# Gated cross-attention with a quantised feed-forward on one core: blocks of tokens as the outer order, groups of heads as the inner one, and split weights kept in DRAM

## The reference, cut to what matters

```python
# x, ctx: 32 sequences x 64 tokens x 512;  32 heads of 128 in 8 groups of 4 heads, one K and V head a group
x = x + tanh(g_xattn) * attn(layernorm(x), ctx)          # causal, softmax over 64 keys
#   Q = xn @ Wq.T (512 -> 4096)   K, V = ctx @ Wk.T, ctx @ Wv.T (512 -> 1024)   y = attn @ Wd.T (4096 -> 512)
x = x + tanh(g_ffn) * (layernorm(x) @ dequant(qweight).T + bias)     # 6-bit weights, 512 -> 512
```

## Time and profile before

| | |
|---|---|
| Time, median of 3 runs | 1126.22 us (1125.69 to 1127.69) |
| Time of the profiled execution | 1125.69 us |
| Span of its profile | 1123.9 us |
| Instructions | 20957 |
| PE busy | 1052.4 us, 94% |
| DVE, ACT, POOL busy | 748.5, 488.8, 109.0 us |
| Mean granted TensorE clock | 0.982 |
| DMA | 53.29 MB, 47 GB/s on average |

### The profile page before, as it was taken

One profiled execution on the slowest core, in us unless ns is written; L12 is line 12 of the kernel. 1 busy time (PEld: TensorE's weight loads), 2 busy tenths in 40 slices (PEclk: granted clock), 3 DMA queues, 4 the chain that ended last, 5 costly groups with the idle time before them and its releaser, 6 DMA issues.

```text
span 1123.9 us, 20957 instructions
## 1 busy us (share of the span) xinstructions
PE 1052.4 (94%) x8060; PEld 594.7 (53%) x8060; DVE 748.5 (67%) x1391; ACT 488.8 (43%) x938; POOL 109.0 (10%) x163
## 2 busy tenths in 40 slices
PE   5799799999999999999999999999999999999985
PEld 2455455555555555555555555555555555555442
DVE  5666467766756566665746666665756576787978
ACT  4666553434433543434433543334433543435342
POOL 1423210000000000000000000000000000003565
PEclk9899899999999999999999999999999999999998
DMA  8140000300021001200021001200022002100111
GB/s 318 58 150 2 19 20 13 101 20 20 20 77 57 20 19 45 76 14 19 20 77 57 20 19 38 79 18 19 20 77 57 20 19 61 35 15 7 38 57 75
DMA packets 46106, 53.29 MB, mean 47 GB/s; under 512 B 3392, under 2 KB 36160, under 8 KB 43584
## 3 DMA queue, kind: packets, MB, share of 16 engines
q1 hardware_dynamic: 46016, 51.92, 15.1%
HBM read 30.93 MB, written 4.19 MB: 31 GB/s over the span
## 4 chain that ended last, share of the span: by engine, by line
PE 77%; DVE 7%; issue 4%; ACT 1%; POOL 0%; DVEq 0%; ACTq 0%; POOLq 0%
PE pa L1085 37%; PE py L1085 27%; PE av L1176 5%; PE ps L1147 3%; PE pp L1161 2%; DVE xacc L894 1%; PE pp L1231 1%; PE pa L1224 1%; PE av L1206 1%; DVE sc L763 1%; DVE row_max L767 1%; DVE q L726 1%; DVE row_sum L776 1%; DVE sc L769 1%; DVE xacc L802 0%
## 5 line engine op out<-in xcount | busy, mean ns | idle before, releaser
L1085 PE MATMUL pa<-xT,wq 128*128 128x512 f16 x1536 | 349.1, 382 | 8.9 <-DVE q L726 5.8
L1085 PE MATMUL py<-wd,att 128*128 128x512 f16 x1536 | 352.1, 382 | 2.2 <-DVE att L793 2.2
L1085 PEld LDWEIGHTS pa<-xT,wq 128*128 128x128 f16 x1536 | 145.4, 99 | 183.4 <-issue 25.9
L1085 PEld LDWEIGHTS py<-wd,att 128*128 128x128 f16 x1536 | 149.1, 98 | 167.2 <-issue 8.1
L525 ACT ACTIVATE q<-pa 128x512 f16<-128x512 f32 x128 | 75.6, 591 | 260.9 <-PE pa L1085 260.9
L802 DVE SCALAR_TENSOR_TENSOR xacc<-py,f_y,xacc 128x512 f32<-128x512 f32 x128 | 96.0, 750 | 134.2 <-PE py L1085 134.0
L569 ACT ACTIVATE att<-av 128x256 f16<-128x256 f32 x256 | 81.0, 385 | 154.3 <-PE av L1176 154.3
L793 DVE SCALAR_TENSOR_TENSOR att<-av,att 128x256 f16<-128x256 f32 x256 | 93.8, 418 | 69.2 <-ACT att L569 69.2
L726 DVE SCALAR_TENSOR_TENSOR q<-pa,q 128x512 f16<-128x512 f32 x128 | 87.7, 685 | 46.0 <-ACT q L525 46.0
L1085 PE MATMUL pa<-wv,cT 128*128 128x128 f16 x1536 | 97.4, 221 | 2.3 <-DVE q L726 2.3
L1085 PEld LDWEIGHTS pa<-wv,cT 128*128 128x128 f16 x1536 | 91.0, 99 | 3.4 <-issue 2.7
(11 more groups left out here) (105 smaller groups left out, 999.2 us busy)
## 6 DMA issues: line engine op xcount, KB each, us to landing
v_dup<-v_nat SPq DMA_DIRECT2D x128, 128.0 KB, 2.4
raw_d<-in_wdT SPq DMA_DIRECT2D x8, 1024.0 KB, 4.9
raw_q<-in_wqT SPq DMA_DIRECT2D x7, 1024.0 KB, 4.9
shared<-in_ctxT SPq DMA_DIRECT2D x4, 1024.0 KB, 6.8
out_x<-xacc SPq DMA_DIRECT2D x16, 256.0 KB, 2.0
xacc<-in_x SPq DMA_DIRECT2D x3, 1024.0 KB, 15.7
raw_k<-in_wkT SPq DMA_DIRECT2D x8, 256.0 KB, 5.1
raw_v<-in_wvT SPq DMA_DIRECT2D x8, 256.0 KB, 5.5
```

What stands on the lines that cost most here:

```text
L1085: last = pe.matmul(out, stationary(a, i), moving(b, i), start=(i == 0 and (a, b) == PASSES[0]), stop=(i == count - 1 and (a, b) == PASSES[ ...
```

## The change

It does five things.

1. **Order.** A pass is one block through all 8 groups; there are four passes, step `n` being group `n % 8` of block `n // 8`. The hardware loop is gone: all 32 steps are written out.
2. **Weights.** Pass 0 loads and splits the weights, now those of the group after the next in each step, and writes the split fp16 tiles to DRAM (`kept_q`, `kept_k`, `kept_v`, `kept_d`). Passes 1 to 3 read them back (`back_qkv`, `back_d`). The sums of squares, the norms and the splits of one group, spread over two steps before, are all in one step.
3. **Blocks.** `xT`, `cT` and `v_dup` hold two blocks, `xacc` three, `c_raw` one. Block `tb + 1` is loaded in step 1 of a pass (`load_block`), its context is squared in step 2, its statistics are taken at the end of step 3, its norm is made in step 4 (`norm_of`), and its context is split in steps 5 and 6.
4. **Feed-forward.** The second norm of a block is in step 0 of the next pass, its feed-forward in step 1 (`ffn_of`); block 2 has it in the last step, block 3 behind it.
5. **Start.** ACT runs an exponential of one column ahead of its first wait. The first norm has four slots of `xn` and `xh` instead of three. The weights of group 1 are prepared ahead of step 0.

```diff
-        def groups(eng, step):
-
-            for tb in range(BLOCKS):
-                step(0, tb, True, False)
-            with eng.Fori(1, GROUPS - 1) as g:
-                for tb in range(BLOCKS):
-                    step(g, tb, False, False)
-            for tb in range(BLOCKS):
...
+        def norm_of(n):
+
+            g, tb = n % GROUPS, n // GROUPS
+            if g == 4 and tb < BLOCKS - 1:
+                return NORMS.index((1, tb + 1))
+            if g == 0 and tb > 0:
+                return NORMS.index((2, tb - 1))
+            return None
...
+        def ffn_of(n):
+
+            g, tb = n % GROUPS, n // GROUPS
+            if n == STEPS - 1:
+                return BLOCKS - 2
+            if g == 1 and 0 < tb < BLOCKS - 1:
+                return tb - 1
+            return None
+
...
+            def keep_qkv(g):
+
+                sp.wait_ge(wq_hi, 4 * (g + 1))
+                sp.wait_ge(wq_lo, 4 * (g + 1))
+                sp.wait_ge(wk_hi, g + 1)
+                sp.wait_ge(wk_lo, g + 1)
+                sp.wait_ge(wv_hi, g + 1)
+                sp.wait_ge(wv_lo, g + 1)
+                sp.dma_start(kept_q[g], wq[:, :, :, :, :].rearrange("p c h k n -> p (c h k n)")).then_inc(q_kept, 16)
+                sp.dma_start(kept_k[g], wk[:, :, :, :].rearrange("p c k n -> p (c k n)")).then_inc(k_kept, 16)
+                sp.dma_start(kept_v[g], wv[:, :, :, :].rearrange("p c k n -> p (c k n)")).then_inc(v_kept, 16)
+
+            def keep_d(g):
+
+                sp.wait_ge(wd_hi, 4 * (g + 1))
+                sp.wait_ge(wd_lo, 4 * (g + 1))
+                sp.dma_start(kept_d[g], wd[:, :, :, :].rearrange("p c h n -> p (c h n)")).then_inc(d_kept, 16)
+
+            def back_qkv(m):
+
+                g = m % GROUPS
+                sp.wait_ge(q_mm, 4 * m)
+                sp.wait_ge(q_kept, 16 * GROUPS)
+                sp.dma_start(wq[:, :, :, :, :].rearrange("p c h k n -> p (c h k n)"), kept_q[g]).then_inc(q_back, 16)
+                sp.wait_ge(k_mm, m)
+                sp.wait_ge(k_kept, 16 * GROUPS)
+                sp.dma_start(wk[:, :, :, :].rearrange("p c k n -> p (c k n)"), kept_k[g]).then_inc(k_back, 16)
+                sp.wait_ge(v_mm, m)
+                sp.wait_ge(v_kept, 16 * GROUPS)
+                sp.dma_start(wv[:, :, :, :].rearrange("p c k n -> p (c k n)"), kept_v[g]).then_inc(v_back, 16)
+
+            def back_d(n):
+
+                sp.wait_ge(y_mm, 4 * n)
+                sp.wait_ge(d_kept, 16 * GROUPS)
+                sp.dma_start(wd[:, :, :, :].rearrange("p c h n -> p (c h n)"), kept_d[n % GROUPS]).then_inc(d_back, 16)
...
+            for n in range(STEPS):
+                g, tb, m = n % GROUPS, n // GROUPS, n + 1
+                if n >= GROUPS:
+                    back_d(n)
+                if tb == 0 and g + 1 < GROUPS:
+                    keep_qkv(g + 1)
+                if tb == 0 and g + 2 < GROUPS:
+                    load_qkv(g + 2)
+                if g == 1 and tb + 1 < BLOCKS:
+                    load_block(tb + 1)
+                if n == GROUPS - 1:
+                    load_ffn()
+                if tb == 0:
+                    keep_d(g)
+                    if g + 1 < GROUPS:
+                        load_d(g + 1)
+                if GROUPS <= m + 1 < STEPS:
+                    back_qkv(m + 1)
+                if m < STEPS:
+                    duplicate_v(m)
+                if ffn_of(n) is not None:
+                    for t in range(ffn_of(n) * TILES, (ffn_of(n) + 1) * TILES):
...
+            squares_q(1)
             k_part(0)
-            ctx_squares(1, 4)
-            v_part(0, 0)
-            squares_d(0, 4)
...
+            squares_kv(1)
+            squares_d(1)
...
+                if tb == 0 and g + 2 < GROUPS:
+                    squares_q(g + 2)
                 p_transposed(n, 0)
+                if tb == 0 and g + 2 < GROUPS:
+                    squares_kv(g + 2, 2 if g == 3 else 0)
                 if ahead:
                     k_part(m)
                 p_transposed(n, 1)
+                if tb == 0 and g + 1 < GROUPS:
+                    squares_d(g + 2)
+                if g == 2 and tb + 1 < BLOCKS:
+                    ctx_squares(tb + 1, squares_done(g + 2) if tb == 0 else squares_done(GROUPS))
                 av_part(n, 0)
...
-                if tb == 1 and not last:
-                    squares_q(g + 1, 0)
+                    v_part(m)
+                if g in (5, 6) and tb + 1 < BLOCKS:
+                    split_ctx(tb + 1, (0, 1) if g == 5 else (2, 3))
                 av_part(n, 2)
-                if reweigh:
+                if tb == 0 and g + 2 < GROUPS:
                     for h in range(HPG):
-                        split_wq(g + 1, h)
-                if tb == 1 and not last:
-                    squares_q(g + 1, 1)
+                        split_wq(g + 2, h)
                 av_part(n, 3)
-                if first and tb < 2:
-                    ctx_squares(tb + 2, 6 + 2 * tb)
-                if tb == 1 and not last:
-                    squares_kv(g + 1, 2 * BLOCKS if first else 0)
-                    squares_d(g + 1)
...
+                if g == 3 and tb + 1 < BLOCKS:
+                    for t in range(TILES):
+                        ln_bn(NORMS.index((1, tb + 1)), t)
+                    ln_stats(NORMS.index((1, tb + 1)))
...
-            def y_unit(g, n, j):
+            def y_unit(n, j):
                 if j == 0:
-                    pe.wait_ge(wd_hi, 4 * (g + 1))
-                    pe.wait_ge(wd_lo, 4 * (g + 1))
+                    if n < GROUPS:
+                        pe.wait_ge(wd_hi, 4 * (n + 1))
+                        pe.wait_ge(wd_lo, 4 * (n + 1))
+                    else:
+                        pe.wait_ge(d_back, 16 * (n - GROUPS + 1))
+                    if ffn_of(n) is not None:
+                        pe.wait_ge(f_scaled, TILES * (ffn_of(n) + 1))
...
+                if tb == 0 and g + 1 < GROUPS:
+                    weight_norms(range(4) if g + 2 < GROUPS else (3,), squares_done(g + 2))
+                if g == 2 and tb + 1 < BLOCKS:
+                    ctx_norm(tb + 1, scale_count(g + 2, 0) if tb == 0 else scale_count(GROUPS, 3))
+                y_unit(n, 0)
```

More of the change, by code:

```diff
@@ new lines, in store @@
+            def store(t):
+                if t in FFN_DVE:
+                    sp.wait_ge(out_dve, FFN_DVE.index(t) + 1)
+                else:
+                    sp.wait_ge(out_pool, t + 1)
+                sp.dma_start(out[t], acc(t)).then_inc(stored, 16)
+            for t in range(TILES):
+                sp.dma_start(xacc[:, 0, t, :], x[t]).then_inc(x0_ld[t], 16)
+            for half in range(2):
+                sp.dma_start(raw_q[:, 2 * half:2 * half + 2, :, :].rearrange("p h k n -> p (h k n)"),
+                             wqT[0][:, half * 2 * D:(half + 1) * 2 * D]).then_inc(wq0_ld[half], 16)
@@ L489, in squares_kv, with squares_q @@
-            def squares_kv(g, c_before=0):
-                act.wait_ge(wkv_ld, 32 * (g + 1))
+                    act.activation(junk[:, :], c_raw[:, 2 * half:2 * half + 2, :].rearrange("p k n -> p (k n)"),
+                                   ACT.Square, accum_out=c_ss[:, half:half + 1]).then_inc(c_ss_ok, 1)
+            def squares_q(s):
+                for half in range(2):
+                    if s > 0 and half == 0:
+                        act.wait_ge(wq_ld, 16 * s)
+                    if s == 0:
+                        act.wait_ge(wq0_ld[half], 16)
+                    wait(act, w_ss_ok, squares_done(s - 1) + half if s > 0 else half)
+                    act.activation(junk[:, :], raw_q[:, 2 * half:2 * half + 2, :, :].rearrange("p h k n -> p (h k n)"),
+                                   ACT.Square, accum_out=w_ss[:, half:half + 1]).then_inc(w_ss_ok, 1)
@@ L629, in step @@
                     q_part(m, 2)
-                if first and tb in (1, 2):
-                    split_ctx(tb + 1, (2, 3))
                 p_part(n, 1)
@@ L664, in step @@
[L664 to L675 removed]
+                if tb == 0 and g + 2 < GROUPS:
+                    split_wk(g + 2)
+                    split_wv(g + 2)
@@ L678, in _, with powers_of_two @@
+                if call is not None:
+                    for t in range(TILES):
+                        ln_hi(TILES * call + t, g == 0)
+                    for t in range(TILES):
+                        ln_out(TILES * call + t)
+            t0 = TILES * (len(NORMS) - 1)
+            for t in range(t0, t0 + TILES):
+                ln_hi(t, True)
+            for t in range(t0, t0 + TILES):
+                ln_out(t)
         @block.vector
         def _(dve):
-            def powers_of_two(norms, exps, pow2, factor, cols, nm, exp_done, pow_done, mul_done, count):
+            def powers_of_two(norms, exps, pow2, factor, nm, exp_done, mul_done, pow_done, count):
@@ new lines, in _ @@
+            weight_scale(1, slice(0, 1))
+            dve.wait_ge(w_mul_ok, 3)
+            dve.wait_ge(q_kept, 16)
```

(43 more changed lines are left out.)

1005 lines of the change are left out of this document (428 added, 577 removed).

## The result

The changed kernel takes 1183.72 us (median of 4 runs, 1180.3 to 1184.51) against 1126.95 for the kernel before (4 runs): ratio 1.0497, interval 1.0472 to 1.0523, 5.0% slower. The profiled execution took 1184.5 us with a span of 1182.7 and a mean granted clock of 0.952.

What follows compares the result with a forecast made beforehand. PE, busy 94% of the span, bounds the kernel, so only its gaps matter. Start 44.4, pass 0 334.1, passes 1 and 2 524.0, pass 3 215.1 and end 59.5 make a span of 1177.1, hence 1179 us; range 1150 to 1203.

Steps and rivals of the forecast that it cites:

- start of step 0: Before step 0: earlier table load and fourth `xn` slot help; group 1's preparation equals block 1's departed norm: 44.4 us.
- passes 1 and 2: 16 plain steps of 30.3 us plus norms, statistics, feed-forwards, context squares and feed-forward weights on DVE: 524.0 us.
- from step 31 to the end: The tail, 70.2 us before, loses 8 of 16 feed-forward units (13.9 us of PE), 3.2 given back: 59.5 us.
- The chain in a preparing step: Pass 0, steps 1 to 6: late `raw_d` load delays squares, attention parts and first output product; 41.4 us a usual step.
- The clock: Pass 0, behind PE's new gap in a preparing step: slower matmuls cost 2.3 us, bounds 1.0 and 3.5.
- Step 0: First step of pass 0: load of `raw_d` issued at T + 14.7, landing at T + 29.9; the step takes 47.4 us.
- Step 4: Pass 0: a usual step plus 2.7 us for statistics ahead of the softmax and 3.0 for a norm: 47.1 us.
- The reads back cost nothing: Passes 1 to 3: reads of kept weights take 4.9 us and fit ahead of their use; a plain step stays 30.3.
- The loop: Removing the hardware loop's turns saves 10.8 us of gaps and 1.5 of slow matmuls: -12.3 us.
- The kept tile does not delay the load: Rival, pass 0: write and read run side by side, seven steps each 2.8 us shorter: 1159 us; chance 0.14.
- the slow writes: Rival, pass 0: writes at half of 370 GB/s, the kept tile takes 2.8 us more seven times: 1199; chance 0.10.
- The rival "faster": Rival, pass 0: a preparing step costs 32.4 us as before, weight work stays hidden: 1117 us; chance 0.07.

Runs made afterwards that it cites:

- late squares: Changed kernel with ACT's squares of `raw_d`, PE's sum and DVE's scale moved to the end of a pass 0 step, one tile kept: 1133.31 us.
- loads first: Changed kernel with the loads of q, k and v ahead of their writes, and `raw_d` ahead of its write: 1168.5 us, ratio 1.0364.
- the other waits taken out: Changed kernel with late squares, loads first, context late, weight squares and statistics moved: 1104.13 us; with step 4's high halves also ahead of ACT's last splits: 1101.32.
- the run with the filled gap: Changed kernel with 18 unread matmuls of 512 columns ahead of PE's weight norms in steps 0 to 6: 1178.63 us, ratio 1.0479.

## Why the prediction was right, point by point

The direction and the size hold, and the mechanism does in steps 1 to 6, though not in step 0: 1179 forecast, 1183.7 measured, a span of 1177.1 against 1182.7. The parts, forecast and measured:

| part | forecast | measured |
|---|---|---|
| start of step 0 | 44.4 | 49.06 |
| pass 0 | 334.1 | 343.63 |
| passes 1 and 2 | 524.0 | 515.31 |
| pass 3 to step 31 | 215.1 | 214.16 |
| from step 31 to the end | 59.5 | 60.54 |

The small total error is partly luck: +14.2 in the first two rows and -8.7 in the third.

- **The chain in a preparing step** stands as worked out. Load issued at T + 16.5 (forecast 16.6), landed at T + 23.55 (23.9), squares ended at T + 25.8 (26.3), first output product at T + 28.5 (27.9). The last is later, although the squares were earlier, because the sums on PE do not hide beside the attention parts: at the lower clock they take 2.72, not 1.3. The clock cost 3.75 in step 1, where I took 2.3; it lay just outside my bound of 3.5. In steps 4 and 5 the same terms make 2.9 and 3.1. Steps 1 and 5 came to 42.3 and 41.5 for 41.4, step 6 to 40.8 for 41.1, step 2 to 45.2 for 43.9, and step 3 to 43.4 for 41.4, where ACT's squares began 8.1 us behind the load's issue, instead of 7.1 in step 1.
- **Step 0** came out near, 48.75 for 47.4, by another path, and that is luck. I had ACT wait for `raw_d`, landed at T + 29.9. But SP's first write went out at T + 16.1, not T + 14.7, and ACT stood 12.06 us at the squares of `raw_q`, which I had said only shift the copies; `raw_d` behind it cost 0.20. The first output product came at T + 37.5, 3.6 later than the forecast's T + 33.9, and the 2.3 that I had for the clock behind it were not paid there (2.75 for the product). With two `raw_d` tiles or late squares of `raw_d` the step stays at 48.2 and 48.5; loads first and the squares of `raw_q` behind the first copy bring it to 41.9.
- **Step 4** is the mis-sized term of pass 0: 47.1 forecast, 51.40. I added the statistics and the norm to a usual step. But the statistics (a wait of 2.14 ahead of the second scores) also push DVE's split of `wd`, and with it the load, which goes out at T + 19.2 instead of 16.5; and the norm has gaps of its own, behind which the clock falls a second time (PE's timeline, T = 228.76):

```profile
234.36 0.86 PE L1129 MATMUL ps<-k,q 128*128 128x64 f16 x24 [2.14 <-DVE sc L755]
...
258.73 2.72 PE L1219 MATMUL pp<-w_ss,ones 128*128 128x1 f32 x12 [6.35 <-ACT junk L480]
261.31 4.39 PE L1055 MATMUL py<-wd,att 128*128 128x512 f16 x12
...
273.00 0.61 PE L1197 MATMUL av<-ident,xh 128*128 128x128 f16 x8 [1.24 <-POOL xh L385]
274.56 0.72 PE L1197 MATMUL av<-ident,xh 128*128 128x128 f16 x8 [0.95 <-issue]
275.07 4.37 PE L1055 MATMUL py<-wd,att 128*128 128x512 f16 x12
```

- **The start** fails at "I set the two equal": the preparation of group 1 was not worth the norm of block 1 that left. The first query product came at 20.95 (forecast 19.1), and then PE waited 6.45 for the squares of `raw_q`, whose load stands behind the writes of group 0. With the loads ahead of the writes step 0 started at 44.53; 0.8 of that is an earlier first query product (20.17), so the writes cost 3.7 there.
- **Passes 1 and 2** were 8.7 shorter. A plain step is 30.20, not 30.3, which is the loop's own cost per step that the rows of before contained (1.6 over 16 steps); the feed-forward weights on DVE, for which I had 3.0, cost 0.4 (33.38 against 32.93 in the step 0 of the two passes); a step with a feed-forward is 6.86 longer, not 8.0; one with a norm and statistics 4.8, not 5.7.
- **The reads back cost nothing**, as forecast: 4.8 us, no wait, and a window over passes 1 to 3 up to step 31 with PE busy for 720.56 of 729.5 us and a clock of 1.00:

```profile
392.70:1122.20 729.50, 720.56 (x5663) 408.09 (x5662) 464.49 (x858) 276.96 (x536) 70.53 (x108) 1.00 0.34 107
```

- **The loop** is worth 16.7, not 12.3, as the kernel before written out shows. The difference is the cost per step in its body, which my list of waits didn't show.
- **The end** lost 9.7 of the 10.7 forecast. Behind the last output product PE waits 11.6 for the last norm (the earlier trace rows had 4.6).
- **The rivals.** "The kept tile does not delay the load" falls: the load took 7.6 beside the write and 5.0 without it, 2.6 of the 2.8 taken. So do the slow writes: 4.8 and 3.9 us for 1 MB. The Trainium skill ("DMA: Bandwidth & Descriptors", Two DMAs through the same engine are not ordered), which I had weighed for the first, speaks of separate read and write sides; the trace shows no full overlap: with the read issued first it took 6.7 and the write 9.3. That page's Bandwidth section has 6.15 us for 1 MB, measured with DMAs that GpSimd issues; the trace here, with DMAs that SP issues, has 5.0 for a load by itself, and the measurement decides. The rival "faster" had the right condition, a preparing step below 33.8 us: the changed kernel misses it at 41 to 51, and the late squares reach it (33.22 in steps 1, 3 and 5) with nothing but a changed order on ACT, PE and DVE.

The waits for `raw_d` in steps 1 to 6 are thus most of the loss: 50.4 of the 56.8 us go when they do. Where the gains that the change makes went can be read off the versions: with the squares late it is still 0.5% slower than before, with the other waits taken out 2.2 to 2.4% faster, and 1.5% is to be had by writing out the loop of the kernel before alone.

## What to carry to other kernels

A tile that lands late cost here what stood behind its consumer in the consumer's queue, not what the transfer took: before buying a second buffer, move the consumer behind the work that the critical engine needs, and look at what then stands behind it at its new place. A write queued beside a load took its share of the rate here whichever was issued first, so a write that nobody waits for belongs well away from a load that somebody does. When a wait is taken out, look at the same step again, since a shorter one is often hidden behind it, and count the lower clock after each gap with it.

## What was unexpected of the hardware

- A step in the hardware loop's body was 0.15 to 0.25 us longer than the same step written out, apart from the 2.2 us at each turn; no list of waits shows it.
- A gap of 2.39 us behind two short ones was enough for PE to drop to the 1.2 GHz level, 5.28 for a product of 2.75. In the run with the filled gap, a gap of 2.63 in step 2 left the sum behind it at full speed (1.50), and the next one, of 3.97 and 5.5 us later, did not.
- A 1 MB write from SBUF to DRAM took 3.9 us from issue to landing (`kept_q`) and 4.4 (`kept_d` well behind the load), less than a 1 MB load (4.8 to 5.0).
